# One stage for each 256-channel deformable layer: corner table and three blocks of offset convolution first, the other blocks' offset convolution between the taps of the gather groups

## The reference, cut to what matters

```python
def deform_conv(x, dw, pw, pwb, w, b):
    f = conv(x, dw, 'SAME', groups=C)          # 7 x 7, depthwise
    off = conv(f, pw, 'SAME') + pwb            # 1 x 1, 18 outputs: 9 taps x (y, x)
    py = yy + ky + off[:, :, 0];  px = xx + kx + off[:, :, 1]
    sampled = bilinear_gather(x, py, px)       # four corners of each tap, zero outside
    return einsum('bckhw,ock->bohw', sampled, w) + b
h = relu(group_norm(x, gn1_g, gn1_b));  h = deform_conv(h, dw1, pw1, pwb1, w1, b1)
h = relu(group_norm(h, gn2_g, gn2_b));  h = deform_conv(h, dw2, pw2, pwb2, w2, b2)
return h + x
```

## Time and profile before

| | |
|---|---|
| median of 3 runs | 6001.1 us (5997.69 to 6001.43) |
| profiled execution, its own time | 5989.28 us |
| its span, first to last instruction | 5987.5 us |
| a 256-channel layer, conv and table stage (first image, layer 0) | 1901.62 to 2035.46 us |
| its corners and first gathers | 2035.46 to 2054.38 us |
| its gather groups | 2054.38 to 2424.55 us |

### The profile page before, as it was taken

One profiled execution on the slowest core, in us unless ns is written; L12 is line 12 of the kernel. 1 busy time (PEld: TensorE's weight loads), 2 busy tenths in 40 slices (PEclk: granted clock), 3 DMA queues, 4 the chain that ended last, 5 costly groups with the idle time before them and its releaser, 6 DMA issues. The chain is left out here.

```text
span 5987.5 us, 83281 instructions
## 1 busy us (share of the span) xinstructions
PE 5187.2 (87%) x24252; PEld 2620.8 (44%) x24252; DVE 4250.2 (71%) x7123; ACT 2265.2 (38%) x4090; POOL 3228.6 (54%) x2826
## 2 busy tenths in 40 slices
PE   7999999997676788878879999999977767888788
PEld 3333333333665544644433333333336655446444
DVE  5888888873223599579858888888732235995798
ACT  2444444441112156235524444444411122662355
POOL 0666666661773277147606666666617732771476
PEclk9999999997787899989989999999977878999899
DMA  1000000001333599579900000000013335995799
GB/s 54 1 1 1 1 1 1 1 1 35 105 105 106 189 410 410 177 272 410 371 32 1 1 1 1 1 1 1 1 37 105 105 110 193 410 410 172 277 410 364
DMA packets 310971, 790.59 MB, mean 132 GB/s; under 512 B 69512, under 2 KB 136401, under 8 KB 310222
## 3 DMA queue, kind: packets, MB, share of 16 engines
q0 software_dynamic: 193536, 679.59, 29.7%
q1 hardware_dynamic: 117198, 107.99, 6.2%
HBM read 701.57 MB, written 85.87 MB: 132 GB/s over the span
## 5 line engine op out<-in xcount | busy, mean ns | idle before, releaser
L615 POOL TENSOR_TENSOR arena<-arena 128x512 f32<-128x512 f32 x960 | 1407.5, 1466 | 828.9 <-ACT arena L1115 764.7
L697 POOL DMA_INDIRECT arena<-corners,arena x1152 | 1086.7, 943 | 993.3 <-POOLq L696 706.7
L1115 ACT ACTIVATE arena<-ps 128x1024 f32<-128x1024 f32 x1024 | 1049.5, 1025 | 1239.2 <-PE ps L840 1209.7
L1564 DVE TENSOR_REDUCE arena<-ps 128x2 f32<-128x1024 f32 x1024 | 1243.3, 1214 | 347.1 <-PE ps L814 347.1
L1046 PE MATMUL ps<-arena 128*128 128x512 f32 x2304 | 1065.3, 606 | 3.3 <-PEq L1043 3.2
L840 PE MATMUL ps<-arena 64*128 64x512 f32 x4096 | 1046.0, 589 | 0.0
L1748 DVE SCALAR_TENSOR_TENSOR ps<-arena,ps 128x256 f32<-128x256 f32 x2304 | 956.9, 483 | 108.1 <-DVEq L1742 69.8
L853 PE MATMUL ps<-arena 128*64 128x512 f32 x4096 | 991.3, 605 | 0.0
L1586 DVE TENSOR_TENSOR arena<-arena 128x512 f32<-128x512 f32 x960 | 890.4, 928 | 62.5 <-ACT arena L1115 62.1
L1269 ACT ACTIVATE ps<-arena 128x256 f32<-128x256 f32 x1152 | 503.1, 469 | 625.4 <-DMA arena<-corners,arena 557.6
L652 POOL DMA_INDIRECT arena<-corners,arena x576 | 546.2, 948 | 338.9 <-issue 173.8
(11 more groups left out here) (132 smaller groups left out, 3708.7 us busy)
## 6 DMA issues: line engine op xcount, KB each, us to landing
corners<-arena SPq DMA_DIRECT2D x256, 256.0 KB, 3.9
arena<-corners,arena POOLq DMA_INDIRECT x1728, 2.8
arena<-in_wd SPq DMA_DIRECT2D x4, 2304.0 KB, 8.3
X<-in_x SPq DMA_DIRECT2D x8, 1024.0 KB, 8.4
corners<-arena SPq DMA_DIRECT2D x128, 64.0 KB, 2.2
out_y<-arena SPq DMA_DIRECT2D x32, 256.0 KB, 5.5
arena<-in_base SPq DMA_DIRECT2D x4, 288.0 KB, 9.2
arena<-in_base SPq DMA_DIRECT2D x2, 432.0 KB, 3.1
```

Of the source, the lines that this page charges most:

```text
L615: pool.tensor_tensor(SUMS[u % 2][:, 0, :], SUMS[u % 2][:, 0, :], P[n % 4][:, 0, :], ALU.add).then_inc(sum_a, 1)
L697: pool.indirect_dma_start(G3[4 * k + t].rearrange("p a c -> p (a c)"), None, table256, bass.IndirectOffsetOnAxis(ap=IS3[:, k, t:t + 1], ax ...
L1115: af(P[n % 4].rearrange("p h q -> p (h q)"), ps[:, 2 * (n % 2):2 * (n % 2) + 2, :].rearrange("p h q -> p (h q)"), ACT.Exp, scale=float(D) ...
L1564: v.tensor_reduce(mxp[i % 2][:, :, j], ps[:, 4:6, :], AX.X, ALU.max).then_inc(mx_done, 1)
```

## The change

Stages 1 to 3 of a layer become one, without a barrier in between. The padded image has rows of 67 words instead of 70 (the right padding of a row is the left one of the next) and is split: `TOP7` holds what blocks 0 to 2 need, `LOW7` what the later ones need. `TS3` has four buffers instead of two.

Ahead of the gathers PE makes all eight `table3` and the convolutions of blocks 0 and 1 between them, then that of block 2. A convolution is now 28 matmuls of 270 or 269 columns in two banks. DVE no longer shifts: ACT copies the 126 rows to SBUF (`raw`), and 7 DMAs issued by ACT (`shift`, 18 partitions x 8 rows x 256 bytes each) write them shifted into `SH3`; PE's `shifted` reads that. `corners` runs for each block by itself (`offsets`: 14 DVE instructions on 72 or 36 columns). POOL's gathers wait for the whole table (`table_ready`), ACT for the corners of block 0.

In the gather groups the convolution of block g+3 runs in group g (g = 0 to 4): 5, 5 and 4 matmuls behind taps 1, 2, 3 and again behind taps 5, 6, 7. Block g+2 (g = 0 to 5) gets `raw` in ACT's tap 1, its shift DMAs in ACT's taps 2 to 5, `shifted` on PE behind tap 4, and `offsets` on DVE behind tap 5. In the second image `wqkv_s` and `wproj_s`, which now lend their space, are loaded again.

```diff
@@ shapes and sync engine
-PW2, PW7 = W + 2, W + 6
+PW2, PW7 = W + 2, W + 3
+AHEAD = 3
...
+                    sp.dma_start(wqkv_s[:], wqkv).then_inc(again_loaded, 16)
+                    sp.dma_start(wproj_s[:], wproj).then_inc(again_loaded, 16)
...
-                    with sp.Fori(0, NCH // 2) as n2:
-                        for p in range(2):
-                            table_writes(p, 2 * n2 + p, TS3[p], table256, C)
-                    for p in range(2):
-                        sp.wait_ge(ts_free[p], 16 * 8)
+                    for n in range(NCH):
+                        table_writes(n % 2, n, TS3[n % NTS], table256, C, ts3_free[n % NTS])
+                    for p in range(NTS):
+                        sp.wait_ge(ts3_free[p], 16 * 8)
+                        sp.sem_inc(ts3_free[p], -16 * 8)
+                    sp.sem_inc(table_ready, 1)
@@ tensor engine
-                    offset_conv(table3, lambda half: HP7[:, half, :], CH, PW7, 7,
-                                lambda half, ky: WO[:, half, ky, :], T3, O3, sel3_s)
+                    def conv(blk, j, first, count, bank):
+                        img, top = (TOP7, 0) if isinstance(blk, int) and blk < AHEAD else (LOW7, AHEAD)
+                        lo, n = (0, HALF7) if j == 0 else (HALF7, BLK7 - HALF7)
+                        for i in range(first, first + count):
+                            half, ky = i // 7, i % 7
+                            last = mm(ps[0:7 * O3, bank, 0:n], WO[:, half, ky, :],
+                                      img[:, half, bass.ds((8 * (blk - top) + ky) * PW7 + lo, n)],
+                                      start=(i == 0), stop=(i == 13))
+                        if first + count == 14:
+                            last.then_inc(conv_ready, 1)
+                    def shifted(bank, col):
+                        pe.wait_ge(shift_in, 16 * 7)
...
+                    table3(0, 0)
+                    table3(1, 1)
+                    pe.wait_ge(image_ready, 2)
...
+                    conv(0, 0, 0, 10, 4)
+                    table3(2, 0)
+                    conv(0, 0, 10, 4, 4)
+                    conv(0, 1, 0, 6, 5)
+                    table3(3, 1)
+                    conv(0, 1, 6, 8, 5)
+                    table3(4, 0)
...
+                    table3(7, 1)
...
+                    shifted(6, 0)
...
+                    conv(2, 0, 0, 14, 4)
+                    conv(2, 1, 0, 14, 5)
+                    shifted(7, 0)
...
+                    def group(g, ahead=False, below=False):
                         for k in range(KK):
                             pe.wait_ge(st_ready, CH)
                             pe.sem_inc(st_ready, -CH)
                             transposes((k + 1) % 3)
                             tap(k)
+                            if below and k == 1:
+                                pe.wait_ge(raw_done, 1)
+                                pe.sem_inc(raw_done, -1)
+                            if ahead and k in (1, 2, 3):
+                                conv(g + AHEAD, 1, (0, 5, 10)[k - 1], (5, 5, 4)[k - 1], 5)
+                            if below and k == 4:
+                                shifted(4, HALF7 + 2)
+                            if below and k == 5:
+                                pe.wait_ge(off_free, 3)
+                                pe.sem_inc(off_free, -1)
+                            if ahead and k in (5, 6, 7):
+                                conv(g + AHEAD, 0, (0, 5, 10)[k - 5], (5, 5, 4)[k - 5], 4)
@@ scalar engine
+                    def raw(bank):
...
+                        af(RAW3[:, 0:HALF7], ps[0:7 * O3, bank, 0:HALF7], ACT.Copy)
+                        af(RAW3[:, HALF7:BLK7], ps[0:7 * O3, bank + 1, 0:BLK7 - HALF7], ACT.Copy).then_inc(act_raw, 1)
...
+                    for n in range(NCH):
+                        norm3(n, n % 2)
+                        if n >= 6:
+                            raw((4, 2)[n - 6])
+                            for kx in range(7):
+                                shift(kx)
...
+                            products(3 * g + t // 3, t % 3, known=(t == 6 and not ends))
+                            if t > 0 or not begins:
+                                staged((t - 1) % 3)
+                            if t == 1 and not begins and layer == 0:
+                                output(g - 1)
+                            if below and t == 1:
+                                raw(4)
+                            if below and 2 <= t <= 5:
+                                for kx in range(2 * t - 4, min(2 * t - 2, 7)):
+                                    shift(kx)
@@ vector engine
+                    for n in range(NCH):
+                        tiles(n)
+                    offsets(0, 6, 0)
+                    offsets(1, 7, 0)
...
+                            sampled(t % 3, 0)
+                            if t == 1 and not begins and layer == 1:
+                                output(g - 1)
+                            sampled(t % 3, 1)
+                            if below and t == 5:
+                                offsets(g + AHEAD - 1, 4, HALF7 + 2)
```

More of the change, by code:

```diff
@@ L349, in _, with table_writes @@
                 n_loads += 6
[L351 removed]
+            def table_writes(p, n, stage, table, cc, free=None):
                 sp.wait_ge(ts_ready, 1)
@@ L1291, in output, with group @@
                                     bias=vec_s[:, B1, oh:oh + 1]).then_inc(evicted, 1)
-                    def three(i, begins=False, evict=None):
-                        for k in range(3):
-                            products(i, k)
-                            if k > 0 or not begins:
-                                staged((k - 1) % 3)
-                            if k == 1 and evict is not None and layer == 0:
-                                output(evict)
+                    def group(g, begins=False, below=False, ends=False):
+                        for t in range(KK):
+                            products(3 * g + t // 3, t % 3, known=(t == 6 and not ends))
[8 more added lines that the diff above has]
+                                    shift(kx)
+                    act.wait_ge(corners_done, 1)
+                    act.sem_inc(corners_done, -1)
                     weights(0, 0)
                     af(IS3.rearrange("p a t -> p (a t)"), IDX3[:, 0:12], ACT.Copy).then_inc(is_ready, 3)
-                    three(0, begins=True)
-                    with act.Fori(1, 3) as k3:
-                        three(k3)
-                    with act.Fori(1, NCH) as g:
-                        three(3 * g, evict=g - 1)
-                        with act.Fori(1, 3) as k3:
-                            three(3 * g + k3)
+                    group(0, begins=True, below=True)
+                    with act.Fori(1, NCH - AHEAD + 1) as g:
+                        group(g, below=True)
+                    with act.Fori(NCH - AHEAD + 1, NCH - 1) as g:
+                        group(g)
+                    group(NCH - 1, ends=True)
                     staged(2)
@@ L1755, in sampled, with group @@
                         dve.sem_inc(chain, -4)
-                    def three(evict=None):
-                        for k in range(3):
-                            sampled(k, 0)
-                            if k == 1 and evict is not None and layer == 1:
-                                output(evict)
-                            sampled(k, 1)
-                    with dve.Fori(0, 3) as k3:
-                        three()
-                    with dve.Fori(1, NCH) as g:
-                        three(evict=g - 1)
-                        with dve.Fori(1, 3) as k3:
-                            three()
+                    def group(g, begins=False, below=False):
+                        for t in range(KK):
+                            sampled(t % 3, 0)
[4 more added lines that the diff above has]
+                                offsets(g + AHEAD - 1, 4, HALF7 + 2)
+                    group(0, begins=True, below=True)
+                    with dve.Fori(1, NCH - AHEAD + 1) as g:
+                        group(g, below=True)
+                    with dve.Fori(NCH - AHEAD + 1, NCH) as g:
+                        group(g)
                     if layer == 1:
```

199 lines of the change are left out of this document (125 added, 74 removed).

## The result

| | before | after |
|---|---|---|
| median of 4 runs each | 5999.4 us (5986.09 to 6001.43) | 6237.7 us (6235.83 to 6245.85) |
| ratio | | 1.0411, 95% interval 1.0398 to 1.0423 |
| profiled execution, own time | 5989.28 us | 6245.85 us |
| first sample to last sample, the four layers | 370.2, 378.7, 369.9, 378.5 us | 497.7, 512.5, 497.2, 511.9 us |
| start of the group norm to first sample | 170.7, 171.5, 170.8, 171.8 us | 101.3, 101.5, 102.5, 100.6 us |

The kernel became some 4% slower (the ratio is the one on record; the two medians alone give 1.0397). The two lower lines of the table say how: the gathers of a layer start 69.7 us earlier on average (279.0 us over four layers), and the gather groups take 522.1 us more. Net 243 us.

What follows compares the result with a forecast made beforehand. PE was taken to bound the conv stage, DMA engines the gather groups. A layer pair costs 222 - 2 x 66 = +90 us, both images +180: 6169 profiled, 6181 as median with 11.8 added; range 6070 to 6290.

Steps and rivals of the forecast that it cites:

- Term 1: Start of a layer's gathers: only the table must be ready, so first sample earlier by 66 us a layer (60 to 74).
- Term 2: PE's work in a gather group with a convolution: 53.3 us against 46.3, so PE becomes the bound.
- Term 3: Detour over DVE behind `shifted`: DVE waits for PE, then PE stands idle 10.2 us in each group.
- term 5: PE's clock falls to 0.50 in the detour's hole, costing 1.0 us a group (0 to 2.3).
- Term 4: Eviction of the previous group's output in tap 1 waits for PE's tap 8: 4.2 us a group (0 to 6).
- The sum of a group: A gather group with convolution and detour: 53.3 + 10.2 + 4.2 + 1.0 = 68.7 us instead of 46.3.
- From the last detour on: End of a layer, from PE's last selections to the last sample, mostly 18 taps at the DMA's rate: 106 us.
- The two layers' growth: First to last sample of a layer: +114 us in layer 0 (484 against 370.2), +108 in layer 1.
- Slower still: Gather groups: ACT's DMA issues or the shifts' landing come late; 6325 us, chance 0.12.
- Milder: Gather groups: the eviction is hidden by DVE's lead and the clock holds; 6066 us, chance 0.13.
- Faster: Gather groups: DVE's detour costs PE nothing, only PE's added work counts; 5890 us, chance 0.07.

Runs made afterwards that it cites:

- e_split_out: Changed kernel with DVE's small offset instructions split, seven each behind taps 7 and 8, and the previous group's output evicted one sample later: 5914.0 us.
- e_ahead4_split_out: e_split_out with one more block done ahead of the gathers (block 3's convolution, block 2's shift, selection and offsets): 5888.2 us, ratio 0.9816.
- e_bare: Changed kernel without any offset work in the gather groups; all blocks gather by the indices and weights of block 0: 5721.5 us.
- e_tap7: Changed kernel with DVE's offsets (the detour) behind tap 7 instead of tap 5: 5960.0 us, ratio 0.9946.
- e_later_out: Changed kernel with the previous group's output evicted one sample later, detour still behind tap 5: 6192.4 us.
- e_early: Changed kernel with PE's selections (`shifted`) ahead of tap 4's matmuls instead of behind them: 6210.6 us.
- e_no_conv: Changed kernel without the convolutions of blocks 3 to 7 in the gather groups: 6061.6 us.
- e_double: Changed kernel with 13 more small DVE instructions in each detour: 6361.9 us.
- e_tap6: Changed kernel with DVE's offsets (the detour) behind tap 6 instead of tap 5: 6081.3 us.
- e_ahead4: Changed kernel with block 3's convolution and block 2's shift, selection and offsets also done ahead of the gathers, detour behind tap 5: 6151.3 us.

## Why the prediction was right, and where its sizes were off

The direction, the mechanism and its place were as forecast; 6181 against 6237.7 us is 57 too little, within the range. The terms that were sized too small are the eviction, the clock and the end of a layer. By its steps:

- **Term 1, the start of the gathers** (66 us a layer): 69.7. The first gather went out 93.8 us behind the start of the group norm (1896.01 to 1989.84) where I had 96.3, and from gather to sample it was 7.5 instead of 7.9. The 64 writes took 66 us with the shifts among them, where I had 66 without and 4 for the shifts. That doesn't make the shifts free: the writes passed at 247 GB/s beside shifts and at 269 in the window behind them, and seven more shifts lengthen the writes by some 3 us (65.34 us to issue in e_split_out, 68.57 in e_ahead4_split_out). What the 14 cost by themselves no run shows, and the 1.5 us for landing had no row behind it. By the rule of the Trainium skill on how a transfer is dealt to engines (DMA: Bandwidth & Descriptors, "Why a DMA increments its semaphore by 16 and not by 1") the prediction estimated the table up to 4 us later still; it came earlier than forecast, and no view shows how many engines carried a shift. The upper bound of 74 was added up wrongly: no shifts and a share of 1.0 make some 77. e_bare confirms the term by itself: its first samples come 279 us earlier over the four layers, less 7.5 us of longer samples are 272, and it ran 269 below the kernel before.
- **Term 2, PE's work in a group** (53.3): 52.3, by the intervals of the PE timeline: nine times 4.31 us for a tap with its transposes, 12.7 for the six pieces, 0.8 for `shifted`.
- **Term 3, the detour** (10.2) **and term 5, the clock** (1.0), together 11.2: 13.4. Tap 5 starts 13.2 us behind the start of `shifted`, where without a hole (e_tap7) it is 1.7, so 11.5; it lasts 1.9 longer. The wait itself was sized rightly, 9.01 + 1.26 against 10.2. DVE's part was 5.9 instead of 5.4. The clock was under-priced: I had read the start of the gathers, where the tap took 4.24 us; behind this hole it took 5.46, and 5.1 on average over all 24, so 1.5 us more than at full clock before the slower transposes are counted.
- **Term 4, the eviction** (4.2 in either layer): 3.5 in layer 0 in the group shown, 6.5 in layer 1. This is the term that was mis-sized most. I let the clock fall once a group; in layer 1 it falls again in the 3.33 us of one-piece idle, which is 2.4 us on the next tap, and in layer 0 in four groups of ten, 1.7 us each. e_later_out takes 3.6 us a group away in layer 1 and 1.1 in layer 0.
- **The sum of a group**: layer 0 52.3 + 13.4 + 3.5 = 69.2 (forecast 68.7), layer 1 52.3 + 13.2 + 6.5 = 72.0 (no forecast of its own).
- **From the last detour on** (106; its parts as named make 104): 113.4 in layer 0. POOL's first gather behind it was issued 10.0 us after the selections ended (2381.6 to 2391.56) and the second 3.0 us later; I had let them run at full rate from 7.8 us on.
- **The two layers' growth** (+114 and +108): +127.5 and +133.9 in the first image. Over four layers that is 78 us more than forecast, less 15 us by which term 1 gained more: 63, and 180 + 63 = 243.

**The rivals.** *Slower still* didn't happen, but it was nearer than its 8 us of room said: I had taken a shift to land within the 2.2 to 3.9 us of the earlier trace rows, and e_early shows 8.3 us among gathers. The wait at L1041 appears as soon as PE is 3.6 us earlier (e_early) or has less to do (e_no_conv, and the last detour of each layer in the changed kernel itself, 1.15 to 2.47 us). The Trainium skill (DMA: Bandwidth & Descriptors, "Queues, rings and completion order") has queues taking turns a packet at a time; the long landing agrees with that, and no run here shows the cause. *Milder* didn't happen: neither the eviction nor the clock was hidden. *Faster* (5890, if the detour costs PE nothing) is not what this program does, for the reason given, the order of the program. With that order changed in one number the kernel does get faster, if by less: 5960 in e_tap7, and 5914 in e_split_out. I had made the condition that `offsets` take 2.4 us or less. That was the wrong condition. The detour kept its length of some 6 us; what had to go was DVE's wait for PE.

What the prediction called "DVE always reaches `offsets` early and waits for PE" is shown to be the cause, by four runs: lengthening the detour costs all of its length (e_double), taking PE's load away leaves the hole as it is (e_no_conv), and moving the detour by one and by two taps takes away 6.1 and 11.2 us a group (e_tap6, e_tap7).

## What to carry to other kernels

An engine that runs ahead of another can keep a lead of as many steps as there are buffers between them (three sample tiles here), and a detour costs the slower engine next to nothing as long as it is shorter than the work that this lead leaves in the slower one's queue (0.37 us of 10.3 in e_tap7). If the detour begins with a wait for the engine behind, the lead is gone before the detour starts and all of it is paid, by the slower engine; so ask for the result as early as possible and read it some steps later, here two taps, which was worth 278 us. Before work is moved under a bound by DMA, sum it up on the engine that gets it (53 us into 46 us here): the groups could never get back to 46, and the change pays only while the sum of these excesses stays below what the start gains, 70 us a layer. And price an idle time with the clock behind it: the tap behind the hole took 1.0 to 2.3 us more than at full clock, and that behind 3.33 us of idling in layer 1 1.8 to 2.7 us more.

## What the runs showed of the hardware

**What an idle time costs in clock.** In layer 1 of the changed kernel PE idles 3.33 us in one piece around an eviction; in all 14 cases the tap behind takes 5.37 to 6.31 us instead of 3.60. In layer 0 it idles 0.32, 0.85 and 1.74 us, with a tap or a few transposes between; the tap behind takes 3.6 us in six cases and 5.3 in four. So the pieces fared better here, but neither their length nor their number decides by itself. In e_early the clock held at all ten of these triples of layer 0; in e_tap7 it fell at all ten, with a tap of 4.79 to 5.30 us behind, as here, after 0.85 and 1.74 us:

```profile
2174.46 4.79 PE L1100 MATMUL ps<-arena 128*128 128x512 f32 x8
```

One piece of 3.0 to 3.1 us ahead of tap 0 left that tap at 3.67 us in all ten groups 1 to 5 of layer 1 in e_later_out, and in three of these ten in e_split_out. What decides stays open.

**A stage that nobody touched moved by 12 us with the clock.** The group norm of layer 0 starts at 1883.68 before and at 1896.01 after. The code up to there is the same. A window of the 64-channel stage, of the kernel before:

```profile
1445.00:1455.00 10.00, 10.00 (x49) 5.56 (x49) 3.83 (x10) 2.88 (x4) 0.00 (x0) 0.83 0.42 78
```

and of the changed kernel:

```profile
1445.00:1455.00 10.00, 10.00 (x32) 5.85 (x33) 4.65 (x13) 0.00 (x0) 0.00 (x0) 0.50 0.40 75
```

From 1445 to 1455 PE is busy without a break in both executions, at a mean clock of 0.83 in one and at the lower level, 0.50, throughout in the other. e_bare and e_split_out start that group norm at 1884.10 and 1883.24, e_ahead4_split_out at 1882.31 and e_ahead4 at 1894.68. The last two of these kernels (with `AHEAD = 4`) are the same program up to there and start it 12.4 us apart, so this comes by execution and not by kernel, and its 12 us are 0.2% of the time. What decides it stays open.
